# Reordering the prologue of an adaLN attention and MoE block: modulation weights in other groups, columns ahead of row statistics

## The reference

```python
mod = (_silu(L0_c) @ L0_wmod).reshape(1, 6, 1, -1)
sa, ca, ga, sb, cb, gb = (mod[:, 0], ..., mod[:, 5])
ga = (2 * (ga >= 0) - 1) * jnp.maximum(jnp.abs(ga), 0.25)   # gb likewise
h = _layernorm(x) * (1 + ca) + sa
x = x + ga * attention(h)        # 16 heads of 128, causal, 2048 keys
h = _layernorm(x) * (1 + cb) + sb
x = x + gb * ffn(h)              # 64 routed experts (top 4) and 2 shared ones
```

## Time and profile before

| | us |
|---|---|
| median of 3 runs | 2029.73 |
| lowest, highest | 2028.84, 2031.98 |
| the profiled execution's own time | 2029.64 |
| its span in the profile | 2027.6 |
| TensorE busy (share of the span) | 1935.7 (95%) |
| VectorE busy | 1418.3 (70%) |
| ScalarE busy | 1122.8 (55%) |
| GpSimd busy | 572.5 (28%) |

### The profile page before, as it was taken

How to read it: one execution, slowest core, us unless ns; L and a number is a source line. 1 busy time by engine, 2 the same in 40 slices (tenths; PEclk the granted TensorE clock), 3 DMA queues, 4 the chain that set the end, 5 groups by cost and what they waited for, 6 DMA issues and landing times.

```text
span 2027.6 us, 33851 instructions
## 1 busy us (share of the span) xinstructions
PE 1935.7 (95%) x9823; PEld 1143.6 (56%) x9825; DVE 1418.3 (70%) x3588; ACT 1122.8 (55%) x1643; POOL 572.5 (28%) x583
## 2 busy tenths in 40 slices
PE   5899999999999999999999999689999999999997
PEld 2444444444444444444444444368877778787786
DVE  5687797797797797797797797646545833333476
ACT  3676776776776676676676686413333144354311
POOL 4531230330330330330330311632000132232265
PEclk8899999999999999999999999799999999999999
DMA  7377777777777777777777777874431098999666
GB/s 241 79 164 176 172 174 176 172 173 176 174 171 176 175 171 176 176 170 176 175 170 176 172 157 161 210 206 143 125 110 32 1 299 283 322 299 306 221 203 186
DMA packets 932181, 366.15 MB, mean 181 GB/s; under 512 B 754800, under 2 KB 885920, under 8 KB 932128
## 3 DMA queue, kind: packets, MB, share of 16 engines
q1 hardware_dynamic: 921888, 331.93, 64.0%
q0 software_dynamic: 10240, 33.56, 5.4%
HBM read 138.86 MB, written 41.94 MB: 89 GB/s over the span
## 4 chain that ended last, share of the span: by engine, by line
PE 72%; DVE 8%; issue 6%; DMA 4%; ACT 3%; POOL 3%; SPq 3%; DVEq 0%; ACTq 0%; POOLq 0%
PE gen L1734 10%; PE gen L1735 10%; PE gen L1736 10%; PE strip L1734 6%; PE strip L1736 6%; PE strip L1735 6%; PE pv L1734 5%; PE pv L1735 5%; PE pv L1736 5%; PE strip L2053 5%; DMA wd_sb<-in_L_ffn_Wd 2%; PE strip L2060 2%; DVE p_lo L1310 2%; SPq L501 2%; DVE exps L1286 1%
## 5 line engine op out<-in xcount | busy, mean ns | idle before, releaser
L955 ACT ACTIVATE exps<-exps,nbias,cols_now 128x128 f32<-128x128 f32 (+15 forms) x256 | 329.8, 1289 | 167.5 <-DVE cmin L1296 165.5
L1310 DVE SCALAR_TENSOR_TENSOR p_lo<-exps,rinv,p_hi 128x512 f16<-128x512 f32 (+3 forms) x256 | 404.9, 1608 | 23.8 <-ACT p_hi L964 23.3
L964 ACT ACTIVATE p_hi<-exps,rinv 128x512 f16<-128x512 f32 (+3 forms) x256 | 333.9, 1352 | 35.1 <-issue 13.7
L1286 DVE TENSOR_SCALAR_CACHE_REDUCE exps<-strip 128x512 f32<-128x512 f32 x384 | 250.9, 687 | 126.5 <-PE strip L1736 123.9
L1734 PE MATMUL strip<-kT_hi,qT_hi 128*128 128x512 f16 (+3 forms) x640 | 221.4, 351 | 28.2 <-DVE kT_lo L1239 16.6
L1734 PE MATMUL pv<-pT,v 128*128 128x512 f16 (+3 forms) x640 | 223.3, 349 | 4.5 <-DMA pT<-p_lo 4.5
L1735 PE MATMUL strip<-kT_lo,qT_hi 128*128 128x512 f16 (+3 forms) x640 | 224.3, 350 | 0.0
L1735 PE MATMUL pv<-pT,v 128*128 128x512 f16 (+3 forms) x640 | 223.3, 349 | 0.0
L1736 PE MATMUL strip<-kT_hi,qT_lo 128*128 128x512 f16 (+3 forms) x640 | 221.7, 350 | 0.0
L1736 PE MATMUL pv<-pT,v 128*128 128x512 f16 (+3 forms) x640 | 219.8, 349 | 0.0
L758 POOL TENSOR_TENSOR wq_f<-wq_f,fac 128x512 f32<-128x512 f32 x15 | 15.6, 1041 | 707.5 <-PE gen L1736 707.5
(11 more groups left out here) (285 smaller groups left out, 4302.1 us busy)
## 6 DMA issues: line engine op xcount, KB each, us to landing
at_dram<-at_f SPq DMA_DIRECT2D x64, 256.0 KB, 2.6
wg_sb<-in_L_ffn_Wg SPq DMA_DIRECT2D x64, 256.0 KB
wu_sb<-in_L_ffn_Wu SPq DMA_DIRECT2D x64, 256.0 KB
wd_sb<-in_L_ffn_Wd SPq DMA_DIRECT2D x64, 256.0 KB
yb_dram<-yb SPq DMA_DIRECT2D x64, 256.0 KB
a_f<-at_dram SPq DMA_DIRECT2D x58, 256.0 KB, 2.8
pT<-p_hi SPq DMA_TRANSPOSE x320, 2.7
pT<-p_lo SPq DMA_TRANSPOSE x320, 2.8
```

The source lines that it names most:

```text
L955: nc.scalar.activation(row, row, ACT.Exp, bias=nbias[:, t:t + 1], scale=cols_now[:, LOGIT_UP:LOGIT_UP + 1], accum_out=rsum[:, t:t + 1]).th ...
L964: nc.scalar.activation(p_hi16[:, 0:j + 1, t, :], row, ACT.Copy, scale=rinv[:, t:t + 1]).then_inc(p_hi, 1)
L1286: nc.vector.tensor_scalar(exps[:, t, 512 * ch:512 * ch + w], strip[u % STRIPS][:, 0:w], 1.0, None, ALU.mult, ALU.max, accum_out=cmax[:, t, ...
L1310: nc.vector.scalar_tensor_tensor(p_lo16[:, 0:j + 1, t, :], row, rinv[:, t:t + 1], p_hi16[:, 0:j + 1, t, :], ALU.mult, ALU.subtract).then_i ...
```

## The change

The first weight group is split in two (`sa`, then `ca`), a third group (`ga`, `sb`) is issued behind x of block 1 with no wait, into `wmod_b`, and the fourth (`cb`, `gb`) after the first two rows, into `wmod_a`. VectorE takes the shift columns ahead of the statistics of block 0, and the scale columns and everything that hangs on them ahead of normalising block 0. TensorE makes the bounds of head 0 ahead of `ln_turn(0)`, then the rows `ga` and `sb` behind it, ahead of "q" of block 0 (ScalarE and GpSimd make h's low part meanwhile). The bounds of head 1 and the row `gb` come between "q" and "k" of block 1, and `cb` ahead of "v". The columns of `sb` and `cb`, the weight sizes, the bounds and the factors of head 1 move up in the lists of VectorE, ScalarE and GpSimd. ScalarE makes three pairs of modulations of block 0 before the first high part of weights.

```diff
-        mod_landed = [... for n in ("sa_ca", "ga", "gb", "sb_cb")]
+        mod_landed = [... for n in ("sa", "ca", "ga_sb", "cb_gb")]
 # SP
-            sp.dma_start(wmod_a[:], wm[:, :, 0:2 * D]).then_inc(mod_landed[0], 16)
+            for n in range(2):
+                sp.dma_start(wmod_a[:, :, n * D:n * D + D], wm[:, :, n * D:n * D + D]).then_inc(mod_landed[n], 16)
             load_x(0)
             for n in range(3):
                 sp.dma_start(raw[n][:], w_dram[n][0]).then_inc(raw_landed[n], 16)
             load_x(1)
+            sp.dma_start(wmod_b[:], wm[:, :, 2 * D:4 * D]).then_inc(mod_landed[2], 16)
             load_x(2)
             load_x(3)
             sp.wait_ge(mod_mm, 3)
-            for n, part in ((1, 2), (2, 5)):
-                sp.dma_start(wmod_a[:, :, (n - 1) * D:n * D], wm[:, :, part * D:part * D + D]
-                             ).then_inc(mod_landed[n], 16)
-            sp.dma_start(wmod_b[:], wm[:, :, 3 * D:5 * D]).then_inc(mod_landed[3], 16)
+            sp.dma_start(wmod_a[:], wm[:, :, 4 * D:6 * D]).then_inc(mod_landed[3], 16)
 # GpSimd
             ln_lo(0)
             ln_scales(0, 1)
-            ln_lo(1, (0, 1))
-            ln_scales(0, 2)
-            ln_lo(1, (2, 3))
 ...
             sizes_of_bias(w_sum).then_inc(w_summed, 1)
+            ln_lo(1, (0, 1))
+            ln_scales(0, 2)
+            ln_lo(1, (2, 3))
             ln_scales(0, 3)
 # ScalarE
-            for ch in range(DC):
-                ln_modulate(0, ch)
-                if ch < 3:
-                    first_hi(ch)
+            ln_modulate(0, 0)
+            ln_modulate(0, 1)
+            ln_modulate(0, 2)
+            first_hi(0)
+            ln_modulate(0, 3)
+            first_hi(1)
+            first_hi(2)
+            take_gate(0)
             gen_hi_of("q", 0, 0)
 ...
             gen_hi_of("v", 0, 0)
+            act.wait_ge(w_bounds, 1)
+            weight_sizes(1)
             for t in range(TB):
                 exp_row(0, 0, t)
-            take_gate(0)
+            gen_hi_of("q", 1, 0)
             take_gate(1)
+            gen_hi_of("k", 1, 0)
             for ch in range(DC):
                 ln_modulate(2, ch)
-            gen_hi_of("q", 1, 0)
-            gen_hi_of("k", 1, 0)
-            act.wait_ge(w_bounds, 1)
-            weight_sizes(1)
 # VectorE
-            ln_stat_of(0)
-
             dve.wait_ge(mod_mm, 2)
             columns(0, gen[0])
-            normalise_x(0)
+            ln_stat_of(0)
             dve.wait_ge(mod_mm, 3)
             columns(DC, gen[1])
 ...
             dve.sem_inc(at_scaled, 2)
+            normalise_x(0)
             take_bounds(0, ...)
 ...
             first_lo(2)
+            dve.wait_ge(mod_mm, 5)
+            columns(3 * DC, gen[1])
+            dve.sem_inc(c_step, 1)
             ln_stat_of(2)
 ...
             row_inverse(0, 0, 3)
+            take_bounds(1, pv[:, 0:3 * P].rearrange("p (n d) -> p n d", n=3))
             ln_stat_of(3)
             gen_out_of("q", 1, 0)
+            gen_out_of("k", 1, 0)
+            factors(1)
             normalise_x(3)
-            gen_out_of("k", 1, 0)
-            dve.wait_ge(mod_mm, 6)
-            columns(3 * DC, pv)
-            dve.sem_inc(mod_out, 1)
             dve.wait_ge(mod_mm, 7)
-            columns(4 * DC, gen[0])
-            scale_of(4 * DC, scale_b)
-            take_bounds(1, pv[:, 0:3 * P].rearrange("p (n d) -> p n d", n=3))
+            columns(4 * DC, pv)
+            link(nc.vector.tensor_scalar(scale_b[:], modT[:, 4 * DC:5 * DC], 1.0, None, ALU.add))
+            dve.sem_inc(c_step, 1)
             for t in range(TB):
                 probs_lo(0, 0, t)
-            factors(1)
 # TensorE
-            ln_turn(0)
             pe.wait_ge(h_bounded, 1)
 ...
                              stop=True).then_inc(w_bounds, 1)
+            ln_turn(0)
+            pe.wait_ge(mod_landed[2], 16)
+            pe.wait_ge(mod_out, 1)
+            mod_rows(pv, wmod_b[:, :, 0:D])
+            mod_rows(gen[1], wmod_b[:, :, D:2 * D])
             project("q", 0, 0)
             ln_turn(1)
+            pe.wait_ge(c_step, 2)
             project("k", 0, 0)
             pe.wait_ge(bound_out, 1)
             project("v", 0, 0)
             pe.wait_ge(ln_mod, 2 * DC)
             score(0, 0)
-            (row ga here)
             project("q", 1, 0)
+            pe.wait_ge(mod_out, 3)
+            (the bounds of head 1, into pv, here)
+            pe.wait_ge(mod_landed[3], 16)
             pe.wait_ge(gen_out, nth("v", 0, 0) + GENS)
             mod_rows(gen[2], wmod_a[:, :, D:2 * D])
             project("k", 1, 0)
             ln_turn(2)
-            (row sb, into pv, here)
+            pe.wait_ge(bound_out, 2)
+            mod_rows(pv, wmod_a[:, :, 0:D])
+            pe.wait_ge(mod_out, 4)
             project("v", 1, 0)
             ln_turn(3)
-            (row cb, into gen[0], and the bounds of head 1, into pv, here)
+            pe.wait_ge(c_step, 3)
             pe.wait_ge(ln_mod, QB * DC)
```

More of the change, by code:

```diff
@@ L293, in adaln_block @@
         c_landed = sem("c_landed")
-        mod_landed = [sem(f"mod_landed_{n}") for n in ("sa_ca", "ga", "gb", "sb_cb")]
+        mod_landed = [sem(f"mod_landed_{n}") for n in ("sa", "ca", "ga_sb", "cb_gb")]
         x_landed = [sem(f"x_landed{b}") for b in range(QB)]
@@ L925, in take_gate @@
             def take_gate(n):
-                act.wait_ge(mod_mm, 4 + n)
+                act.wait_ge(mod_mm, (4, 6)[n])
                 nc.scalar.activation((ga_bc, gb_bc)[n][:], (pv, gen[2])[n][:], ACT.Copy).then_inc(mod_out, 1)
@@ L1225, in columns @@
                 link(nc.vector.tensor_reduce(modT[:, first:first + DC], tmp, AX_X, ALU.add))
-            def scale_of(first, dst):
-                link(nc.vector.tensor_scalar(dst[:], modT[:, first:first + DC], 1.0, None, ALU.add))
-                dve.sem_inc(mod_out, 1)
             def gen_out_of(kind, j, h):
@@ L1839, in _ @@
             mod_rows(gen[0], wmod_a[:, :, 0:D])
+            pe.wait_ge(mod_landed[1], 16)
             mod_rows(gen[1], wmod_a[:, :, D:2 * D])
-            ln_turn(0)
             pe.wait_ge(h_bounded, 1)
@@ L1856, in _ @@
             score(0, 0)
-            pe.wait_ge(mod_landed[1], 16)
-            pe.wait_ge(mod_out, 1)
-            mod_rows(pv, wmod_a[:, :, 0:D])
             project("q", 1, 0)
-            pe.wait_ge(mod_landed[2], 16)
-            pe.wait_ge(gen_out, nth("v", 0, 0) + GENS)
-            mod_rows(gen[2], wmod_a[:, :, D:2 * D])
-            project("k", 1, 0)
-            ln_turn(2)
-            pe.wait_ge(mod_landed[3], 16)
-            pe.wait_ge(mod_out, 4)
-            mod_rows(pv, wmod_b[:, :, 0:D])
-            project("v", 1, 0)
-            ln_turn(3)
-            pe.wait_ge(gen_out, nth("q", 1, 0) + GENS)
-            mod_rows(gen[0], wmod_b[:, :, D:2 * D])
-            pe.wait_ge(mod_out, 5)
+            pe.wait_ge(mod_out, 3)
             pe.wait_ge(abs_ready, 2)
@@ L1878, in _ @@
             weight_bounds(1, pv, False)
+            pe.wait_ge(mod_landed[3], 16)
+            pe.wait_ge(gen_out, nth("v", 0, 0) + GENS)
+            mod_rows(gen[2], wmod_a[:, :, D:2 * D])
+            project("k", 1, 0)
+            ln_turn(2)
+            pe.wait_ge(bound_out, 2)
+            mod_rows(pv, wmod_a[:, :, 0:D])
+            pe.wait_ge(mod_out, 4)
+            project("v", 1, 0)
+            ln_turn(3)
+            pe.wait_ge(c_step, 3)
             pe.wait_ge(ln_mod, QB * DC)
-            pe.wait_ge(mod_out, 6)
-            pe.wait_ge(bound_out, 2)
             with pe.Fori(0, H - 2) as h:
```

1 line of the change is left out of this document (removed).

## The result

The changed kernel took 2025.22 us (median of 12 runs, 2022.03 to 2029.43) against 2029.74 for the kernel before beside it: a ratio of 0.9977, 95% interval 0.9966 to 0.9988, or 2.4 to 6.9 us less. It is faster by 0.2%, and 2024.0 was forecast. The medians are 4.5 us apart, where 5.6 were foreseen. The profiled execution took 2022.86 (span 2021.1), 6.8 less than the one before it; it is the fourth quickest of its twelve, and that of before lies at the median, so the 6.8 flatter the change somewhat.

The account below looks back on a forecast made before the run. The start of TensorE's unbroken work, 84.39 us, was taken to set the end. Modulations of block 3 (-2.6) and the tail (-3.0) gave -5.6 us against 2029.64: 2024.0, own range 2022.5 to 2025.9, with rivals 2021.0 to 2028.8.

Parts of the forecast that it names:

- The start: Prologue, TensorE: with two 1 MB groups the first row starts near 7.75 us, the second ends at 17.2.
- The columns ahead: VectorE, block 0: bounds 2.3 us earlier, at 21.1; normalising ends at 26.1, ScalarE starts near 26.5 instead of 24.61.
- The clock and the two rows: TensorE's hole before "q" of block 0: rows fill it to 36.9, "q" ends at 39.5, only 0.1 us later.
- One row less ahead of the last transposes, bounds more: TensorE, -2.45 us: transposes could start at 67.2; modulations of block 3 at 68.7 instead of 71.26, -2.6.
- The tail: From block 3's modulations to the score row of stage (0,1): 9.35 us instead of 12.38, -3.0; row at 78.05.
- the first rival: Clock up sooner, across the hole (2021.5 us) or, second half, at the strips of (0,1) (2021.0); chance 0.14.
- `wmod_b` landed in time: Rival: `wmod_b` lands only with the backlog's end at 34.3, "q" ends at 46.3, +6.8 us: 2030.8; chance 0.07.
- the low clock did not hold through the rows and "q": Rival: low clock holds there, "q" ends at 47.6, +8.1 us: 2032.1, or 2039 if it lasts longer; chance 0.04.
- the gain was still there at the end: Rival: a later transfer or another engine eats the gain, 2029.6 us; chance 0.03.
- The stalls did not stack: Rival: p_lo on VectorE waits for POOL's gate steps three times, +4.6 us, 2028.6 (half: 2026.3); chance 0.10.

Follow-up runs that it names:

- the repeat: The changed kernel run once more, unchanged, against the kernel before: ratio 0.9965 (0.9952 to 0.9977), median 2022.97 us of 8 runs, span 2020.0.
- the repeat of before: The kernel before profiled once more, unchanged, a single execution: span 2025.6 us, scores of (0,2) at 98.11.
- early filler: Changed kernel plus five fp32 products that feed nothing, behind row `ca` on TensorE: ratio to before 0.9968 to 0.9991, span 2021.9 us.
- filler late: Changed kernel plus five idle products behind the last transposes, ahead of the strips of stage (0,1): ratio to before 0.9964 to 0.9991, span 2027.1 us.
- rows out: Changed kernel with rows `ga` and `sb` moved from ahead of "q" to behind scores (0,0): median 2033.69 us, ratio to before 1.0003 to 1.0024.
- one 2 MB group: Changed kernel with `sa` and `ca` in one 2 MB transfer again: median 2027.57 us, ratio to before 0.9970 to 0.9990.
- GpSimd waits: Changed kernel with GpSimd's three raw-weight products held until block 0 is normalised: median 2023.06 us, ratio to before 0.9951 to 0.9976.
- gate late: Changed kernel with GpSimd's gate steps held until ScalarE's first result of attention: median 2027.87 us, ratio to before 0.9972 to 0.9994.
- columns back: Changed kernel with normalising and turning block 0 again ahead of the scale columns and bounds: ratio to before 0.9967 to 0.9991, span 2021.7 us.

## Why the prediction held, step by step

- **The start.** First product 7.89 (7.75 foreseen), second row done at 17.5 (17.2). The group of 2 MB put back moved all by 2.7, the term's own size. Right.
- **The columns ahead.** Bounds matmul at 21.96, not 21.1: `h_bound` took 0.80 us and VectorE reached it later; beside GpSimd's `w_sum` it was held up, a stall that the step did not have. It cost nothing more, for four normalisings beside GpSimd took 2.87 us, where alternation would have had 3.9. They ended at 26.4 (26.1), ScalarE began at 27.03 (26.5).
- **The clock and the two rows.** The clock fell at 20, the rows ran from 29.28 to 36.54 (28.9 to 36.9), the rise came at 30, and "q" ended at 39.13 (39.5). Right in each part, with the rise about a microsecond sooner than the 31.1 of the sum. Luck is in it as well: "q" ended at 38.03 to 39.86 in kernels with the same work up to there. The reason given for the low clock was misread, though it did no harm: at 84.39 in the earlier trace rows the clock was low not from the 2.21 us of standstill ahead of it but since 80.2, where it fell with TensorE at work (the product at 80.11 took 0.58 already). `wmod_b` was issued at 11.16 and landed 12.2 us later, at 23.4, well ahead of 29.3. The 21.6 foreseen added 2.1 MB of one unit (a million bytes) to 4.75 of another (2^20 bytes): in one unit it is 7.1 MB and 22.2 us. That the rows in the hole are nearly free was the main claim, and taking them out lost the gain: shown.
- **One row less ahead of the last transposes, bounds more.** Transposes could start at 67.2 by the sum; they started at 66.55. Of the 0.65 us, 0.24 are sooner first scores, 0.18 the bounds (0.82 us, not 1.0), and most of the rest is VectorE's wait that the 69.62 of before held (TensorE was free at 69.33). And the normalising that was to end at 68.3 ended at 66.6 (4.42 us for four beside GpSimd: between the free 1.91 and the alternating 5.6). This is the term that was mis-sized: the modulations of block 3 began at 67.19, 1.5 sooner than 68.7 and 0.5 sooner than the lower bound of 67.7. -4.1 came of it instead of -2.6.
- **The tail.** 9.50 us from there to the score row (9.35 foreseen, 12.38 before): 76.69, -6.95 instead of -5.6.
- **What was not foreseen.** A wait of 2.40 us (0.92 in the repeat) for the transposed probabilities took the place of VectorE's. In the trace of before it was 0, because the score row was last. With the row 7 us sooner, the four transposes in SP's queue, which hang on p_hi, are late next. The prediction passed the whole shift of the row on to TensorE: it only asked who waits for VectorE, not which other input of the same products would be late next. That gap in the reasoning cost the forecast nothing that can be seen. From the score row to the scores of (0,2) are 15.5 and 15.3 us in the two traces of before, 16.0 and 14.8 in the two of the changed kernel. The kernel before had waits and slow clock of its own in that stretch, and that they weigh as much as the new wait is luck.

In numbers, for the first pair of traces: the row came 6.95 sooner. From it to the weighted values were 5.52 us before and 5.93 after, 3.53 without the wait; the values themselves took 1.64 instead of 2.25. That is 7.15 at "q" of the next step, 6.5 at the scores of (0,2), and 6.5 at the end, against the 5.6 of the sum. It looks as if the clock had given 2.0 us and the wait taken 2.4. But in the repeat of before, with the clock up at 82, the row to the values is 3.22 us and the values take 1.63: the sooner clock at the strips, the second half of the first rival, comes and goes without the change and can't be booked to it. What holds in both pairs is the row (6.95 and 6.39 sooner), the scores of (0,2) (6.5 and 6.9) and the end (6.5 and 5.6).

The other rivals did not come: `wmod_b` landed in time, the low clock did not hold through the rows and "q", and the gain was still there at the end. The stalls did not stack either: p_lo lost 0.4 us of 3.48 to GpSimd, against 4.6 in that rival. The Trainium skill (SBUF — State Buffer, "Who interferes with whom") says that a VectorE tensor_scalar in a 2-port mode, and a VectorE instruction with two SBUF inputs beside a GpSimd one that reads SBUF, contend with GpSimd: one of the two is blocked for the whole instruction of the other. For the normalising tensor_scalar the trace agrees in kind (four take 2.87 us beside, 1.91 alone, and 3.9 if they alternated in full). For `mod_scale`, with two small inputs, it agrees in full: it ended at 23.04, with GpSimd's product (21.98 to 23.02). For p_lo the measurement decides otherwise (3.48 beside the gate steps, 3.13 without).

Left open: the median gain is 4.5 us (2.4 to 6.9) in one set and about 7 (0.9965, that is 4.7 to 9.7) in the other, on the same code. The profiled executions show why a narrower figure isn't had: the stretch from the first to the last result of attention (ScalarE's first and last copy of it) took 1248.9 to 1252.7 us in the kernels of the table, and what is behind it 680.6 to 688.4. What makes these differ from run to run was not traced. How the worth of the clock's rise at the strips divides from that of the transposes stays open too: the filler at either place gave no time that can be told from none.

## What to carry to other kernels

A standstill of an in-order engine is worth as much as independent work can be put into it: here two rows of products left the end of "q" where it was, within its spread of 1.8 us, and cost 6.9 where they stood on the path. Part of why they fit is the clock: with them ahead "q" took 2.6 us at full clock, without them 3.9 to 5.0. When a wait is shortened by several microseconds, list every input of the instructions behind it with its own time; the second latest is the new bound (here four transfers in series, not the engine that was watched). And where runs of one kernel differ by more than an edit is worth, read marks inside the trace just behind the edit, take the difference of two marks that the chance ahead of them cancels from, and profile the unchanged kernel twice before believing one mark.

## What the runs showed of the hardware that was not expected

- The clock fell while TensorE was at work, though after a stretch with waits in it. With the early filler TensorE was busy for 0.59 us of 22 to 24, 1.02 of 24 to 26 and all of 26 to 28, on the bounds and then on transposes, and the granted clock was 1.00, 0.86 (it fell at 25.4) and 0.50. In the kernel before it fell at 80.2, 0.9 us into the strips; in its repeat at 78.6.
- Its fall is not at a fixed place: in two kernels with the same instructions up to there, the granted clock at 20 to 22 us was 0.50 (changed) and 0.93 (filler late), and the four bounds products took 1.46 and 1.03 us. The end of "q" ranged from 38.0 to 39.9 in kernels with no edit ahead of it; how much of that is the clock alone is not shown.
- A VectorE instruction of 4 elements a partition can be held up as long as a large one: 1.02 us instead of 0.16 beside GpSimd's products, to within 0.02 us of the end of the product that ran beside it.
- A DMA transpose on SP is mostly issued in 1.24 us, but one of four took 1.98 to 2.42 us in several kernels (changed, rows out, one 2 MB group, filler late, GpSimd waits, gate late). The last one's landing varied too, from 2.75 us behind its issue to 5.45. The wait of TensorE hangs on both, and on how soon the strips are done: 0 with a slow issue (filler late), 2.57 with none (columns back), 3.58 with both late (gate late).
